# Where one-hot supertiles stand in two edge layers of a graph network, and how their tables are built

## What is computed

```python
edge_index = jnp.stack([src, dst])
h = relu(layernorm(x));  x = x + L0(h, edge_index, ...)            # six graph convolutions and a small MLP
h = relu(layernorm(x));  x = x + L1(h, src, dst, edge_type_8, ...) # typed layer
h = relu(layernorm(x));  x = x + L2(h, edge_index, ...)            # one graph convolution
h = relu(layernorm(x));  x = x + L3(h, edge_attr_16, ..., src, dst, edge_type_90)

# typed layer (L1), 8 edge types: the messages, before a GRU update
A = edge_emb[edge_type].reshape(-1, 16, 16)
msg = jnp.einsum('emh,eh->em', A, features[edge_src])
m = jax.ops.segment_sum(msg, edge_dst, num_segments=6250)

# relation layer (L3), 90 relations
W_rel = jnp.matmul(w_comp, V).reshape(90, 16, 16)
e = jnp.concatenate([z_src, z_e, z_dst], axis=1) @ Wa.T
msg = jnp.einsum('ei,eio->eo', h[src], W_rel[rel_type]) * e
h_out = jax.ops.segment_sum(msg, dst, num_segments=6250)
```

## Time and profile before

| | us |
|---|---|
| median of 3 timed runs | 4047.14 |
| lowest and highest | 4045.97, 4049.79 |
| the profiled execution | 4036.76 |
| its span, first to last instruction | 4031.9 |

### The profile page before, as it was taken

The page is one execution under the profiler, slowest core; times in us unless marked ns, Lnnn a source line. Parts: engine busy times, 40 slices in busy tenths (PEclk is TensorE's granted clock), DMA queues, the critical chain, the costliest instruction groups (busy, mean ns, idle before and its releaser), DMA issues. The chain is left out here.

```text
span 4031.9 us, 75830 instructions
## 1 busy us (share of the span) xinstructions
PE 3457.1 (86%) x28016; PEld 1995.6 (49%) x28016; DVE 2704.4 (67%) x6568; ACT 1168.9 (29%) x2300; POOL 1976.3 (49%) x1875
## 2 busy tenths in 40 slices
PE   3677776699999996999999999368999999999995
PEld 2455555355445553555555555134565555555553
DVE  7999999222222112888887877326998777787785
ACT  1555555000110000444443444025222222222221
POOL 0000000583000000777777777226777777777775
PEclk7999999799999997999999999677999898988997
DMA  5333333874515448233322222578322222222222
GB/s 172 60 60 78 71 60 59 339 296 165 223 57 224 179 169 299 56 64 64 64 62 58 60 59 52 175 298 316 71 50 52 43 43 45 41 48 43 43 48 32
DMA packets 482431, 443.65 MB, mean 110 GB/s; under 512 B 370419, under 2 KB 420077, under 8 KB 470793
## 3 DMA queue, kind: packets, MB, share of 16 engines
q1 hardware_dynamic: 393200, 390.75, 31.3%
q0 software_dynamic: 56208, 34.21, 6.5%
q10 hardware_dynamic: 32650, 13.77, 1.3%
HBM read 344.31 MB, written 95.88 MB: 109 GB/s over the span
## 5 line engine op out<-in xcount | busy, mean ns | idle before, releaser
L1589 POOL DMA_INDIRECT rows<-typed_table,ring x640 | 738.1, 1153 | 204.7 <-issue 194.8
L1255 PE MATMUL L_ps<-ring,L_T 128*128 128x448 fp8e4 (+1 forms) x4704 | 682.6, 395 | 86.0 <-DMA ring<-adj 54.5
L1963 PE MATMUL l_ps_g<-ring,h_part 128*128 128x512 f16 (+1 forms) x2436 | 619.0, 388 | 0.0
L536 PE MATMUL cells<-keys,lows 128*128 128x294 f16 (+4 forms) x2744 | 389.3, 286 | 194.8 <-DVE keys L512 178.1
L1933 POOL DMA_INDIRECT ring<-typed_table,l_idxA x432 | 473.7, 1097 | 158.7 <-issue 129.6
L1255 PEld LDWEIGHTS L_ps<-ring,L_T 128*128 128x128 f16 (+1 forms) x4704 | 332.6, 107 | 422.4 <-issue 86.5
L1933 POOL DMA_INDIRECT l_rows<-typed_table,l_idxA x400 | 444.5, 1111 | 122.0 <-issue 120.1
L512 DVE TENSOR_SCALAR keys<-build_or_wx,recs 128x294 f16<-128x294 f16 (+4 forms) x1960 | 462.1, 312 | 0.0
L1264 DVE SCALAR_TENSOR_TENSOR L_Y<-L_ps,L_scale,dinvB 128x448 f32<-128x448 f32 x98 | 66.9, 683 | 574.2 <-PE L_ps L1255 574.1
L536 PEld LDWEIGHTS cells<-keys,lows 128*128 128x128 f16 x2744 | 287.1, 141 | 295.6 <-DVE keys L512 283.3
L1617 ACT ACTIVATE sel<-ps_g 128x512 f16<-128x512 f32 x488 | 291.5, 597 | 440.2 <-PE ps_g L1612 440.2
(11 more groups left out here) (319 smaller groups left out, 4384.9 us busy)
## 6 DMA issues: line engine op xcount, KB each, us to landing
ring<-adj SPq DMA_DIRECT2D x69, 2744.0 KB, 10.5
adj<-ring SPq DMA_DIRECT2D x14, 2744.0 KB, 8.8
typed_table<-ring SPq DMA_DIRECT2D x49, 765.0 KB, 5.1
ring_fifth<-src_div_mod_rows SPq DMA_DIRECT2D x122, 256.0 KB
l_krow<-src_div_mod_rows SPq DMA_DIRECT2D x87, 256.0 KB
l_trow<-type_row SPq DMA_DIRECT2D x98, 180.0 KB
attr<-in_he POOLq DMA_DIRECT2D x25, 512.0 KB, 8.0
klast<-last_keys SPq DMA_DIRECT2D x81, 128.0 KB
```

Source lines behind the costliest of these rows:

```text
L536: ins = pe.matmul(to, lows[g // QG % 3][:, :, g % QG * KT + j], keys[g % OB][:, j, (a1 - a) * NT:(b1 - a) * NT], start=j == FIRST[h], stop ...
L1255: ins = pe.matmul(bank[at:at + rows, 0:CH], d["T"][q][:, k, 0:rows], ring[r][:, k, :], start=n < side, stop=n >= NT - side, tile_position= ...
L1589: r_tok_[g] = r_in[b].by(pool.indirect_dma_start(rows[b][:, j, :], None, t1_dram, bass.IndirectOffsetOnAxis(ap=idxA[:, k * SUP + j:k * SUP ...
L1963: ins = pe.matmul(ps_g[p][:, 0:HE], parts[p][0:m, j, :], hot[b][0:m, j, h * HE:(h + 1) * HE], start=j == 0, stop=j == GJ - 1)
```

## The change

Both layers now end with three one-hot supertiles (`TAIL` = 3), and the tables' share is spread over the supertiles between the lead and these: 78 in place of 80 in the typed layer, 103 in place of 104 in the relation layer. So there are two more one-hot supertiles in the first and one more in the second (88 in place of 87). The typed table gets a staging buffer for each of its 13 stores (the new ones lie in the unused part of `dinvB`), so no copy waits; DVE waits for all stores ahead of its second `make_hot`, whose block lies on those buffers. The relation table gets 7 staging buffers in place of 3; four of them lie where the one-hot blocks go, so the first two `make_hot` of that layer wait for the last stores. DVE takes the middle eviction of the first 12 tiles, and in turns 1 to 10 one tile stands before `expand`, one in the middle of it and two behind `messages`, in place of two and two. A semaphore is saved by counting one store of L0 on another.

```diff
-LEAD1, DIRECT1, ROWS_AHEAD = 3, 80, 12
-PLAIN, LEAD, DIRECT = 11, 2, 104
+LEAD1, DIRECT1, ROWS_AHEAD = 3, 78, 12
+PLAIN, LEAD, DIRECT = 11, 2, 103
+TAIL = 3
+FIRST_TILES = 12
...
-            kinds = ["table" if k >= LEAD1 and (k - LEAD1 + 1) * DIRECT1 // (SG - LEAD1) > (k - LEAD1) * DIRECT1 // (SG - LEAD1) else "matmul" for k in range(SG)]
+            mixed = SG - LEAD1 - TAIL
+            kinds = ["table" if 0 <= k - LEAD1 < mixed and (k - LEAD1 + 1) * DIRECT1 // mixed > (k - LEAD1) * DIRECT1 // mixed else "matmul" for k in range(SG)]
...
-            stage = [spare[:, 2 * ET + b * SE // 2:2 * ET + (b + 1) * SE // 2].bitcast(F32).rearrange("p (t c) -> p t c", c=P) for b in range(4)]
+            pieces = [spare[:, 2 * ET + b * 4 * P:2 * ET + (b + 1) * 4 * P].bitcast(F32) for b in range(4)]
+            pieces += [dinvB[:, at:at + 4 * P] for at in (*range(GJ * KK * F, half - 4 * P + 1, 4 * P), *range(half + SE, NP - 4 * P + 1, 4 * P))]
+            stage = [x.rearrange("p (t c) -> p t c", c=P) for x in pieces] + [dinvB[:, NP - P:].rearrange("p (t c) -> p t c", c=P)]
...
             dve.wait_ge(*table_made)
+            dve.wait_ge(s_tab.sem, s_tab.n)
             dve.wait_ge(*split_tok)
...
-            stage = [flat[3].bitcast(F32)[:, i * XC:(i + 1) * XC] for i in range(3)]
+            stage = [flat[r].bitcast(F32)[:, i * XC:(i + 1) * XC] for r, i in ((3, 0), (3, 1), (3, 2), (0, 0), (1, 0), (0, 1), (1, 1))]
+            ST = len(stage)
...
             def table_tile(m):
                 bank3 = [ps_g[0], ps_g[1], ps_f]
-                if m >= 3:
-                    act.wait_ge(s_tab[m % 3].sem, 16 * (m // 3))
                 for j in range(3):
                     c = slice(j * XC // 3, (j + 1) * XC // 3)
                     if m:
                         pe.wait_ge(*tab_tok[m - 1, j])
...
+                    if m < FIRST_TILES and j == 1:
+                        dve.wait_ge(*tok)
+                        if m >= ST:
+                            dve.wait_ge(*stored_tok[m - ST])
+                        tab_tok[m, j] = c_x.by(dve.tensor_copy(stage[m % ST][:, c], bank3[j][:, 0:XC // 3]))
+                    else:
+                        act.wait_ge(*tok)
+                        if m >= ST and j == 0:
+                            act.wait_ge(*stored_tok[m - ST])
+                        tab_tok[m, j] = c_tab.by(act.activation(stage[m % ST][:, c], bank3[j][:, 0:XC // 3], ACT.Copy))
...
                     if i >= 2 and by_matmul[i - 2]:
                         dve.wait_ge(*gat[i - 2, HALVES - 1])
+                    else:
+                        for m in range(NT - ST, NT):
+                            if m % ST >= 3:
+                                dve.wait_ge(*stored_tok[m])
...
-            def expand(i):
+            def expand(i, between=()):
                 pe.wait_ge(*ty_tok[i])
                 for q in range(SUP // 2):
+                    if q == SUP // 4:
+                        for m in between:
+                            table_tile(m)
...
-                for m in tiles[:2]:
+                ahead = 1 if 1 <= i < PLAIN else len(tiles)
+                for m in tiles[:ahead]:
                     table_tile(m)
...
-                    expand(i - 1)
+                    expand(i - 1, tiles[ahead:ahead + 1])
...
-                for m in tiles[2:]:
+                for m in tiles[ahead + 1:]:
                     table_tile(m)
```

More of the change, by code:

```diff
@@ L1509, in typed_layer @@
             s_all, s_index = Counted(nc, "types_in"), Counted(nc, "index_in")
-            s_tab = [Counted(nc, f"table_out{b}") for b in range(4)]
+            s_tab = Counted(nc, "table_out")
             k_in, r_in, o_out = keys_in, rows_in, sums_out
@@ L1522, in typed_layer @@
             act.wait_ge(*blank)
+            assert len(stage) == -(-NT // 4)
             iota_ready = step(pool, pool.iota(iota8[:, :], pattern=[[1, R8]], base=0, channel_multiplier=0))
@@ L1809, in relation_layer @@
             termA = dinvB[:, NP // 2:NP // 2 + ET]
-            kinds = ["plain" if k < PLAIN else "matmul" if k < PLAIN + LEAD else
-                     "table" if (k - PLAIN - LEAD + 1) * DIRECT // (SG - PLAIN - LEAD) > (k - PLAIN - LEAD) * DIRECT // (SG - PLAIN - LEAD)
+            first, mixed = PLAIN + LEAD, SG - PLAIN - LEAD - TAIL
+            kinds = ["plain" if k < PLAIN else
+                     "table" if 0 <= k - first < mixed and (k - first + 1) * DIRECT // mixed > (k - first) * DIRECT // mixed
                      else "matmul" for k in range(SG)]
@@ L1843, in relation_layer @@
             s_all = Counted(nc, "l3_edges_in")
-            s_tab = [Counted(nc, f"l3_table_out{i}") for i in range(3)]
+            s_tab = [Counted(nc, f"l3_table_out{i}") for i in range(ST)]
             k_in, r_in, o_out = keys_in, rows_in, sums_out
@@ L1895, in table_tile @@
                         pe.wait_ge(*tab_tok[m - 1, j])
[L1896 to L1899 removed]
+                    tok = c_t.by(pe.matmul(bank3[j][:, 0:XC // 3], HxT[:, m * P:(m + 1) * P], wx[:, c], start=True, stop=True))
+                    if m < FIRST_TILES and j == 1:
[8 more added lines that the diff above has]
+                        tab_tok[m, j] = c_tab.by(act.activation(stage[m % ST][:, c], bank3[j][:, 0:XC // 3], ACT.Copy))
+                for j in range(1, 3):
+                    sp.wait_ge(*tab_tok[m, j])
+                stored_tok[m] = s_tab[m % ST].by(sp.dma_start(t3_dram[m * P * R90:(m + 1) * P * R90, :].rearrange("(p r) c -> p (r c)", p=P), stage[m % ST]), 16)
             def load_edges(i):
@@ L1925, in fetch_table_rows @@
                     pool.wait_ge(*index_ready)
-                    for m in range(NT - 3, NT):
-                        pool.wait_ge(s_tab[m % 3].sem, 16 * (m // 3 + 1))
+                    for m in range(NT - ST, NT):
+                        pool.wait_ge(*stored_tok[m])
                 if g >= RT:
@@ L2060, in put_sums @@
                 o_out[h].by(act.dma_start(m3_dram[bass.ds(base, WIN), h, :], sums[h][at, :]), 16)
-            TILES = [0] + [12 + 4 * i for i in range(PLAIN - 1)] + [NT]
+            TILES = [0] + [FIRST_TILES + 4 * i for i in range(PLAIN - 1)] + [NT]
             load_edges(0)
```

19 lines of the change are left out of this document (5 added, 14 removed).

## The result

The changed kernel took 4034.88 us (median of 20 runs, 4026.46 to 4048.11) beside 4049.26 us for the kernel before (20 runs, 4042.34 to 4062.73): ratio 0.9966, 95% interval 0.9956 to 0.9976, so 14 us faster (10 to 18). Forecast were 11.3 us. On another chip of the same kind it came again: 4030.81 against 4048.34 us, 0.9958 (0.9943 to 0.9974). The profiled execution took 4039.11 us. The traces are therefore compared stage by stage, each from its own start.

What follows compares the result with a forecast made beforehand. POOL's gathers were taken to set the pace in both edge layers. Typed layer -15.6 and relation layer +4.3 summed to -11.3 us, from the median of 4047.14 to 4035.8 us, range 4026 to 4050.

Steps and rivals of the forecast that it cites:

- (1): Typed layer's gathers: 16 fewer at 1.26 us, two more one-hot supertiles +2.1, together -18.1 us.
- (4): Relation layer's gathers: 8 fewer at 1.26 us, one more one-hot supertile +1.4, together -8.7 us.
- hangs on the one-hots: Both layers: gather time above 1.26 us apiece charged to one-hot supertiles, 1.04 us each typed, 1.42 relation.
- (2): Typed layer's start: with 13 buffers copies no longer wait and stores follow each other, POOL starts earlier, -2.5 us.
- (3): Typed layer's end: last rows' sum now stands ahead of the last fold, whose chain follows, +5.0 us.
- (5): Relation layer's end: three one-hot supertiles queued behind the last `weigh_rows`, covered by nothing, +27.0 us.
- (6): Relation layer's start: table rebuilt faster with 7 buffers, turns of some 9.7 us, -14 us.
- the bound of -18: Relation start's far end: 49 stores transferred without a gap, 111 us from 2698.7, worth -18 us.
- The rivals that rested on PE at 1.2 GHz: Relation table rebuild: 1.2 GHz in most turns, 4044.8 us, chance 0.30; in every turn, 4055.8 us, chance 0.08.
- The semaphore saved: Counting one store on another's semaphore costs nothing, since its store is long done: 0 us.
- Covered tails: Both layers' ends: PE and DVE ahead, terms 3 and 5 near nothing, -43 us, 4004; chance 0.06.
- -19.2: Whole kernel: the sum without the port-sharing rule, removed gathers priced at the mean, 34.7 us, in place of -11.3.

Runs made afterwards that it cites:

- the run without tails: Changed kernel with no closing one-hot supertiles (TAIL = 0), 78 and 103 tables spread to the end: 4013.45 us, 0.9915 against the kernel before.
- the compares' run: Changed kernel with five of six DVE compares left out from each buffer's third one-hot supertile on: 3958.97 against 4043.78 us for the kernel before, 0.9780.

## Why the prediction was right

It said -11.3 us and the result is -14. Its premise holds: POOL sets the pace, with no gap between its gathers in the kernel before, in the changed one and with fewer tables, and the relation layer's gathers end sooner as soon as each is cheaper. Step by step:

- **(1) and (4), gathers, -18.1 and -8.7.** Over-sized, clearly so in the relation layer. On one chip three tables less gave -14 by the medians, -17 with 8 to either side by the means; in the traces -9.7 (932.4 to 922.7) and -5.9 (1174.0 to 1168.1). Over four tables in each layer the rate is 7.0 and 7.7 us a table, against 9.0 and 8.7 forecast. The step that failed is the excess that "hangs on the one-hots": 1.04 and 1.42 us for each were means over the layer. One more one-hot supertile adds more: 8 x 1.26 = 10.1 less 7.0 and 7.7, 3.1 and 2.4 us. In the relation layer the traces show how: the gathers over 1.75 us are 62 and 64 with 104 tables, 69 to 72 with 103, 73 with 100. They grow faster than the one-hot supertiles do, 87, 88 and 91. In the typed layer the changed kernel's second trace, at 906.2, shows that the scatter of this term (some 16 us) is as large as the term, so there 3.1 can't be told from 1.04.
- **(2) Typed start, -2.5.** Nothing. From the first table store to POOL's first gather are 18.8 us before, 18.2 and 19.2 now. The copy's wait of 5.37 us was read as time in which the transfers could have gone faster. They could not: in the stretch ahead of the first gather the DMA engines are busy in nearly all slices of both kernels. The first line of each is before's, from 1588 to 1604.7 in 40 slices, then after's, from 1590 to 1608:

```profile
DMA  9999999699999979537999999999999999999595
```

```profile
DMA  9999999999998999999999499999999999999975
GB/s 260 206 124 113 100 84 106 47 44 74 193 179 166 310 316 313 312 314 275 302 203 174 173 355 336 329 342 342 338 346 346 345 346 346 344 348 359 302 123 155
```

  The store's price of 0.7 us for 256 KB is right for its best part (345 GB/s are 0.76 us), but the first third of the stretch moves 130 GB/s in the mean, and eight slices of it no more than 44 to 124. I took the price from stores of another table and let them have the engines to themselves.
- **(3) Typed tail, +5.0.** 5.5 by the trace (3.6 to 9.1), by the chain named.
- **(5) Relation tail, +27.0.** 26.9 (2.9 to 29.8). The reading of one late table in the middle carried over whole.
- **(6) Relation start, -14.** 19.3 us in the trace; by the stretch from the first plain fetch to the first table gather 13 to 18 in the six traces with the new table, 15 in the mean. The turn takes 9.2 us, not 9.7 (before 10.86, by the transfers 8.9). The 19.3 lie beyond the bound of -18, but that bound was added up wrongly: 2698.7 + 111 is 21 us ahead of 2831.08. The rivals that rested on PE at 1.2 GHz fall. `expand` is slow in both halves in one of ten (2.72 us for 12 multiplies at 2727.02, 1.47 in most others) and nearly so in the last (4.66 for 24); the turn of the first took 9.06 us, no more than the rest. In the trace of before it was slow in four of ten. The granted clock from 2712 to 2798 is 0.90, from 2722 to 2820 it was 0.79. What this higher clock gave to the term is not separated.
- **The semaphore saved, 0.** No cost can be read. POOL's first instruction of the typed layer starts at 1573.4 us in the trace of before and at 1573.9 to 1579.3 in the six with the saving on this kind of chip; in the two without it on the other kind it starts at 1576.1 and 1577.6.
- **Covered tails**, the rival of -43, is refuted: the run without tails is faster, by 19 us in the medians and 27 at the relation layer's end.

So the total came out so near partly by luck: two misses nearly cancel in it, gathers worth 13 us less than said by the medians and tails costing 13 less. The two are not independent. Both are taken from the time of the kernel without tails, and up to some 8 us of each can be the error of its five runs. At the relation layer's end the tail stands in full, 27 us, in both traces; the other 5 of the 32 were seen in the chain and not won back without it. The mechanisms named were those that ran, but for the copies' wait in (2). The sizes were known to some 5 us a term, no better.

The Trainium skill's rule that spoke against the change (SBUF — State Buffer, "Who interferes with whom") moved the sum the right way, from -19.2 to -11.3. It tells nothing of the size, and the compares' run shows that the effect is there. The Trainium skill (DMA: Bandwidth & Descriptors, "Queues, rings and completion order") has the descriptors of a queue taken in ring order on each DMA engine. The turns above agree, where the type row comes behind the stores: from the third on DVE waits 1.7 to 3.1 us for it in each.

## What to carry to other kernels

Where one engine sets the pace, price the next unit of work at what it adds, not at the mean of the layer, look at which single instructions of that engine are long and what runs beside them, and look at what a run with four units moved says before trusting one with a single unit. Work of another kind placed behind the last piece of the pacing engine is a tail in full: of this change's parts the three closing supertiles were the one that cost, and the same kernel without them and with fewer tables is 79 us faster than before. A wait in front of a transfer is only worth its length if the DMA engines are idle in it.

## What was not expected of the hardware

- The same kernel takes 4044 to 4049 us on some chips and 4823 to 4874 on others. Up to 1573 us the two traces agree, and again in L2; in the layers with POOL's indirect transfers many of PE's instructions start 0.7 us apart with nothing to wait for, and the granted clock in the typed layer is 0.83 in place of 0.97. A gain measured on one kind of chip does not carry over to the other: three tables less were worth 0.4% on the first kind and 2.7% on the second.
- Two traces of one kernel can differ by 16.7 us in 624 gathers (1.452 and 1.479 us apiece), while the next layer's 824 agree to 0.5 us.
- Leaving out five of six compares on DVE shortened 824 gathers on POOL by 67.5 us, with PE and transfers as they were. A gather beside the products and reduces of `messages` costs what it costs alone, 0.944 us; most of the excess sits in 70 gathers of 2.34 us, at the ends of `make_hot`.
